# Loading the conditional matrix A from GpSimd's DMA queue instead of ScalarE's

## What is computed

```python
# x (32, 128, 2048), W0 (16, 128, 128), W1 (8, 2048, 2048), all float32
W = W0[itok_B_0_15]                       # one 128x128 matrix A per sequence
x = x + einsum('bct,bcd->bdt', x, W)
w = W1[itok_B_3_7]                        # one 2048x2048 matrix per sequence
x = x + einsum('bsi,boi->bso', x, w)
```

## Time and profile before

| | |
|---|---|
| time, median of 3 runs | 1533.56 us (1533.41 to 1533.66) |
| span of the profiled execution | 1532.7 us |
| PE busy | 1489.7 us |
| DVE busy | 1012.1 us |
| ACT busy | 503.3 us |
| POOL busy | 968.6 us |
| PE from 50 us to 1460 us after the start | busy all but about 5 us |

### The profile page before, as it was taken

The page is one execution under the profiler, slowest core; times in us unless marked ns, Lnnn a source line. Parts: engine busy times, 40 slices in busy tenths (PEclk is TensorE's granted clock), DMA queues, the critical chain, the costliest instruction groups (busy, mean ns, idle before and its releaser), DMA issues.

```text
span 1532.7 us, 28812 instructions
## 1 busy us (share of the span) xinstructions
PE 1489.7 (97%) x6534; PEld 1227.5 (80%) x6535; DVE 1012.1 (66%) x617; ACT 503.3 (33%) x778; POOL 968.6 (63%) x650
## 2 busy tenths in 40 slices
PE   2799999999999999999999999999999999999998
PEld 1688788888888888887888888888888888888887
DVE  5979752859597693293958878257677797528521
ACT  2322333333333333333333332332333333333332
POOL 2576666666676766666566666667666667566653
PEclk9999999999999999999999999999999999999999
DMA  8989885889798896596979989569798998848543
GB/s 161 196 186 205 174 188 119 177 179 188 161 198 184 173 212 149 122 188 148 207 159 204 190 181 202 132 144 191 166 185 187 187 203 183 178 110 180 120 112 88
DMA packets 280411, 261.26 MB, mean 170 GB/s; under 512 B 17748, under 2 KB 197972, under 8 KB 280404
## 3 DMA queue, kind: packets, MB, share of 16 engines
q10 hardware_dynamic: 110592, 176.21, 50.0%
q1 hardware_dynamic: 169812, 84.97, 31.1%
HBM read 227.56 MB, written 33.55 MB: 170 GB/s over the span
## 4 chain that ended last, share of the span: by engine, by line
PE 86%; DMA 8%; ACTq 2%; issue 1%; DVE 1%; ACT 1%; POOL 1%; SPq 0%; DVEq 0%; POOLq 0%
PE z_ps L542 27%; PE z_ps L533 27%; PE z_ps L532 27%; DMA a_full<-in_L_cond_weights 6%; PE out_ps L554 2%; PE out_ps L551 2%; PE out_ps L552 2%; ACTq L160 1%; DMA w_nat<-in_L_cond_weight 1%; ACTq L149 1%; DVE w_turn L427 0%; POOL a_full L218 0%; DMA x_nat<-in_x 0%; ACT x_high L258 0%; DVE w_nat L420 0%
## 5 line engine op out<-in xcount | busy, mean ns | idle before, releaser
L532 PE MATMUL z_ps<-w_high,x_high 128*128 x2032 | 790.4, 389 | 0.0
L533 PE MATMUL z_ps<-w_low,x_high 128*128 x2032 | 790.4, 389 | 0.0
L207 POOL TENSOR_TENSOR x_low<-x_turn,x_high 128x1024 fp32r<-128x1024 f32 x256 | 667.0, 2626 | 22.8 <-ACT x_high L258 22.8
L437 DVE STREAM_TRANSPOSE x_turn<-x_nat 128x1024 f32<-128x1024 f32 x258 | 306.0, 1222 | 466.4 <-DMA x_nat<-in_x 463.8
L542 PE MATMUL z_ps<-w_high,x_low 128*128 x2032 | 481.4, 389 | 0.0
L533 PEld LDWEIGHTS z_ps<-w_low,x_high 128*128 128x128 f32 x2032 | 381.4, 188 | 79.2
L532 PEld LDWEIGHTS z_ps<-w_high,x_high 128*128 128x128 f32 x2032 | 381.4, 188 | 79.2
L542 PEld LDWEIGHTS z_ps<-w_high,x_low 128*128 128x128 f32 x2032 | 381.4, 188 | 79.2
L218 POOL TENSOR_TENSOR a_full<-a_full,ident 128x128 f32<-128x128 f32 x128 | 74.3, 581 | 338.4 <-DMA a_full<-in_L_cond_weights 338.4
L258 ACT ACTIVATE x_high<-x_turn 128x1024 fp32r<-128x1024 f32 x256 | 257.4, 1060 | 17.7 <-DVE x_turn L437 17.5
L474 DVE TENSOR_TENSOR w_low<-w_turn,w_high 128x2048 fp32r<-128x2048 f32 x76 | 252.1, 3317 | 2.6
(11 more groups left out here) (69 smaller groups left out, 190.5 us busy)
## 6 DMA issues: line engine op xcount, KB each, us to landing
x_nat<-in_x ACTq DMA_DIRECT2D x512, 256.0 KB, 5.2
w_nat<-in_L_cond_weight SPq DMA_DIRECT2D x320, 256.0 KB, 7.7
out<-out_sb ACTq DMA_DIRECT2D x128, 256.0 KB, 6.1
a_full<-in_L_cond_weights ACTq DMA_DIRECT2D x128, 64.0 KB, 5.1
x_nat<-in_x SPq DMA_DIRECT2D x4, 256.0 KB, 4.9
ids_row<-in_itok_B SPq DMA_DIRECT2D x1, 16.0 KB
cond_i<-in_itok_B SPq DMA_DIRECT2D x1, 0.5 KB
```

Of the source, the lines that this page charges most:

```text
L207: nc.gpsimd.tensor_tensor(x_low[s][:, half], x_turn[:, half], x_high[s][:, half], ALU.subtract)\
L437: nc.vector.transpose(x_turn[:].rearrange("p (k a c) -> p k a c", a=QUAD, c=SQ)[:, blocks], x_nat[:].rearrange("p (a k c) -> p k a c", a=Q ...
L532: nc.tensor.matmul(z_ps[s][:], xs, w_high[:, ds(at + k * NC, NC)], start=(k == 0), stop=False)
L533: nc.tensor.matmul(z_ps[s][:], xs, w_low[:, ds(at + k * NC, NC)], start=False, stop=False)
```

## The change

The function `load_a` moves from ScalarE's program to GpSimd's. There it stands right behind `a_parts(t - 1)`, which ends with the instruction that frees `a_full`, and ahead of `z_rest(t - 1)`. In ScalarE's program the wait for `a_split`, the register load and the DMA issue are gone. The first load stands ahead of GpSimd's first `x_rest`, behind a wait for the tables.

```diff
@@ gpsimd
+            def load_a(t):
+
+                pool.wait_ge(a_split, t)
+                c = by_step(pool, COND, t, w0.shape[0] - 1)
+                pool.dma_start(a_full[:], w0[ds(c, 1), :, :].rearrange("o c d -> (o c) d")).then_inc(a_loaded, DMA)
+
...
+            pool.wait_ge(tables_made, 2)
+            load_a(0)
             x_rest(0, 0)
...
                     t = 2 * p + (2 - s)
+                    load_a(t)
                     z_rest(t - 1)
                     x_rest(t + 1, 1 - s)
                     a_parts(t)
+            load_a(STEPS - 1)
             z_rest(STEPS - 2)
             a_parts(STEPS - 1)
@@ scalar
-            def load_a(t):
-                c = by_step(act, COND, t, w0.shape[0] - 1)
-                act.dma_start(a_full[:], w0[ds(c, 1), :, :].rearrange("o c d -> (o c) d")).then_inc(a_loaded, DMA)
...
                     load_x(t + 2)
-                act.wait_ge(a_split, t)
-                load_a(t)
                 take_out(t - 1, 1 - s, stored)
                 take_a(t)
...
             act.wait_ge(tables_made, 2)
-            load_a(0)
             take_x(0, 0)
```

## The result

The changed kernel took 1550.78 us (median of 4 runs, 1548.69 to 1552.02) beside 1533.49 us for the kernel before on the same chip: a ratio of 1.0113, with a 95% interval of 1.0101 to 1.0125. The forecast was 1529.0 us, in a range of 1527.5 to 1535.5. The profiled execution has a span of 1550.3 us, 17.6 us more than before.

A forecast was written before the change was run, and what follows sets the result against it. The prediction took TensorE to bound the kernel, losing 6.48 us in the loop. From 1532.7 us, -6.0 for the early load and +1.4 for the first step gave 1528.1, plus 0.9 to the runs' median: 1529.0 us, range 1527.5 to 1535.5.

The forecast's parts named there:

- What bounds: Whole kernel: TensorE bounds, busy 1489.7 of 1532.7 us; other engines' changes give back only what TensorE waits.
- a purse of 6.48 us: Loop: TensorE's loss over 126 steps against 11.56 us a step, the most the change could win there.
- ScalarE, and the load in the loop: Loop: ScalarE's saved work counted for nothing; A's earlier load removes nearly all late steps, -6.0 us.
- The issue on POOL: POOL ahead of `z_low`: table entry and DMA issue cost 1.4 us, between 0.64 and 4.3, hidden in quiet steps.
- the 3 us named as a sign of being wrong: Each step: `z_low` starting over 3 us behind the end of `a_low` would show the forecast wrong.
- The first step: Start of the loop: no cover, so TensorE's first L554 comes later by the whole issue, +1.4 us.
- The very first load: Ahead of POOL's first `x_low`: covered by 5.9 us, costed at nothing; `x_low` after 16.5 us would show it wrong.
- The rule that speaks against it: VectorE's fast-form cast locks out GpSimd's descriptor writing, so the load looks blocked; most of the gain would be lost.
- The first, a dear issue: POOL's issue costs 3 us instead of 1.4 and takes back part of the gain: 1531.6 us, chance 0.18.
- The second, a late landing: VectorE's cast holds up the load, which lands in 7 or 8 us: 1534.3 us, chance 0.14.
- The third, POOL as the bound: POOL bounds the loop from an issue of 3.53 us on, each further microsecond costing 127 us; slower, chance 0.10.
- the other signs named: Profile after: TensorE waiting for `z_low` beyond the first step would refute; ScalarE's wait for POOL's sum nearly vanishing would confirm.

The follow-up runs named there:

- act_early: The kernel before with ScalarE's wait for `a_split` and its load of A moved ahead of its next loads of x; 1529.11 us, ratio 0.9972.
- z_first: The changed kernel with one swap on GpSimd, `z_rest(t - 1)` ahead of `load_a(t)`; 1526.64 us, ratio 0.9959 to the kernel before.
- after_psum: The changed kernel with the identity that VectorE's L423 reads kept in PSUM instead of SBUF; 1528.83 us, ratio 0.9973 to the kernel before.
- delay3: The kernel before with three table entries loaded for nothing on GpSimd between `a_low` and `z_low`; 1555.94 us, ratio 1.0151.

## Why the prediction was wrong, step by step

**What bounds.** Right. TensorE's rhythm and a purse of 6.48 us in the loop: act_early and z_first collected 5.4 and 6.3 us of it.

**ScalarE, and the load in the loop, -6.0 us.** The load did what was expected of it: landed in 3.3 us at the median instead of 5.1, POOL's wait for it fell from 338.4 us to none (under 60 was forecast). The -6.0 us are real as an effect of an early load (5.4 us in act_early, 6.3 in z_first), but the sum took them for the whole effect on the loop. **This is the step that failed:** the list of who waits behind POOL's issue named `z_low` and TensorE and stopped there. VectorE in the loop was never priced, which put it at nothing without a reason. It shares a port with POOL that no semaphore shows, and L423 went from 54.0 to 185.8 us. The loop lost 14.9 us where 6.0 were to be won.

**The issue on POOL, 1.4 us.** Mis-sized. `z_low` starts 1.89 us behind the end of `a_low`: 1.3 us for the wait and the table entry, and 0.56 us for the DMA instruction. The bounds of 0.64 and 4.3 us held, and the 3 us named as a sign of being wrong were not reached.

**The first step, +1.4 us.** Right in kind, and paid with 2.80 us: 1.97 us for `z_low` behind `a_low` and 0.83 us by which this execution's start was later already. The stretch at the lower clock behind it, 1.4 us more, had no term at all. after_psum, whose VectorE isn't held at the start, has the first L554 at 58.08, with the issue at the same place.

**The very first load, at nothing.** The first `x_low` starts at 16.8 us instead of 16.5. The prediction had called that a sign of being wrong; it is worth 0.3 us.

**The rule that speaks against it.** The hold by VectorE's cast exists and is small. Timeline of the changed kernel:

```profile
144.16 1.23 DVE L475 CAST w_high<-w_turn 128x2048 fp32r<-128x2048 f32 x1
144.31 1.20 POOL L219 DMA_DIRECT2D a_full<-in_L_cond_weights  x1 [1.34 <-issue]
145.43 3.56 DVE L477 TENSOR_TENSOR w_low<-w_turn,w_high 128x2048 fp32r<-128x2048 f32 x1
```

The DMA instruction takes 1.20 us instead of 0.56 and ends 0.12 us behind the cast. The instruction's 128 executions sum to 83.5 us, 12 us above 128 times the shortest, and the load is wanted much later. The rule of the Trainium skill (SBUF — State Buffer, section "SBUF: two separate sides") holds as far as this trace goes, and its worth here was near nothing; what cost the time runs the other way, from GpSimd's work to VectorE.

**The rivals.** The first, a dear issue, had 3 us for a price that was 1.9; after_psum pays the same 1.9 us and loses 1.7 us in the loop, so it isn't what took the gain. The second, a late landing, didn't come about. The third, POOL as the bound, ends on the right side, and its threshold of 3.53 us was wrong: it was made from means, and delay3 reaches it at 1.91 us in the steps where `x_low` takes 7.8 us. In the changed kernel itself it isn't the mechanism, since after_psum has the same POOL issue and loses 1.7 us. I had given 0.15 to slower and had noticed, in one sentence, that the cast and POOL "seem to wait for one another"; the same look at the two-input L420 (0.24 us at the least, 2.53 at the most, in the kernel before) would have shown that VectorE's and POOL's times depend on how they meet. Of the other signs named, TensorE's wait for `z_low` outside the first step came (15 waits with the first), and ScalarE's wait for POOL's sum didn't nearly vanish (197.8 us).

## What to carry to other kernels

When work is added to an engine, list not only who waits for it by semaphore but who shares a port with it: an instruction whose shortest and longest times differ by a factor of ten at one shape is the sign, and its sum belongs among the terms. Where a DMA stands in GpSimd's program matters to VectorE's two-input work: here the place between `z_low` and `x_low` instead of ahead of both was worth 24 us, because 54 of VectorE's 80 sums began during `z_low` and were let in at its end. And slack made from mean busy times hides the steps in which an instruction is stretched, so a threshold is better worked out from the longest round that the trace shows.

## What the runs showed of the hardware that was not expected

A 0.25 us instruction of VectorE with two SBUF inputs can be held for up to 6.58 us, through three or four instructions of GpSimd, when the first of them follows a DMA instruction of GpSimd at once; in the three kernels of the table without such a DMA it is held through one, for 1.43 us at the most when it begins during `z_low`. A load of 64 KB from GpSimd's queue landed in 3.3 us at the median, and in 5.1 us from ScalarE's, where it was issued behind 1 MB of x; in act_early, ahead of x on ScalarE's queue, it landed in 2.6 us, so it is the place in the order and not the queue that made it faster. And on GpSimd a table entry with its register work, loaded for nothing, costs about 0.55 us a piece (2.46 against 1.91 us for four and three), nearly twice its 0.29 us in the profile.
